# Experts' second layer two pairs of tiles behind the first, with three buffers of h1

## What is computed

```python
x = x + tanh(g_xattn) * attention(ctx, layernorm(x), ctx, mask)
h = layernorm(x) * gamma + beta
shared_out = silu(h @ sw1.T) @ sw2.T
probs = softmax(h @ router_w.T)
best, gate = argmax(probs), max(probs)
routed_out = gate * (silu(h @ ew1[best].T) @ ew2[best].T)
x = x + tanh(g_ffn) * (shared_out + routed_out)
```

## Time and profile before

| | us |
|---|---|
| median of the three runs | 543.09 |
| lowest and highest | 540.36, 544.48 |
| the profiled execution | 543.73 |
| its span, first to last instruction | 541.7 |
| TensorE, VectorE, GpSimd, ScalarE busy in it | 507.2, 435.5, 373.8, 316.1 |
| mean granted clock of TensorE | 0.979 |

### The profile page before, as it was taken

One profiled execution on the slowest core, in us unless ns is written; L12 is line 12 of the kernel. 1 busy time (PEld: TensorE's weight loads), 2 busy tenths in 40 slices (PEclk: granted clock), 3 DMA queues, 4 the chain that ended last, 5 costly groups with the idle time before them and its releaser, 6 DMA issues.

```text
span 541.7 us, 21366 instructions
## 1 busy us (share of the span) xinstructions
PE 507.2 (94%) x8178; PEld 427.4 (79%) x8178; DVE 435.5 (80%) x1257; ACT 316.1 (58%) x711; POOL 373.8 (69%) x828
## 2 busy tenths in 40 slices
PE   6899999999999999999999999999979889999991
PEld 2578677878878788888888888887768879999990
DVE  7688878888898888888777777787677888898971
ACT  3435355555556556666565655645559867777770
POOL 7267888677686777877778677685652777666663
PEclk9799999999999999999999999999979999999996
DMA  6935041020210202112021020200310434232110
GB/s 159 216 105 148 14 136 50 14 59 27 75 56 28 65 25 76 42 43 65 24 76 46 26 65 13 70 12 11 87 47 26 117 105 107 76 85 75 38 40 10
DMA packets 53427, 34.66 MB, mean 64 GB/s; under 512 B 6002, under 2 KB 50750, under 8 KB 53328
## 3 DMA queue, kind: packets, MB, share of 16 engines
q1 hardware_dynamic: 48000, 24.52, 17.1%
q0 software_dynamic: 4320, 8.53, 4.6%
q10 hardware_dynamic: 1008, 0.25, 0.2%
HBM read 24.16 MB, written 9.59 MB: 62 GB/s over the span
## 4 chain that ended last, share of the span: by engine, by line
PE 67%; DVE 16%; POOL 4%; issue 4%; ACT 3%; DMA 2%; SPq 1%; ACTq 0%; POOLq 0%; DVEq 0%
PE PS L1247 11%; PE PS L1215 8%; PE PS L1198 8%; PE PS L1228 7%; PE PS L1185 5%; PE PS L1274 5%; PE PS L1452 5%; PE PS L1456 4%; PE PS L1440 3%; PE PS L1433 3%; DVE nm L629 3%; DVE rinv L637 3%; PE PS L1206 1%; PE PS L1168 1%; PE PS L1285 1%
## 5 line engine op out<-in xcount | busy, mean ns | idle before, releaser
L1016 ACT ACTIVATE shared<-PS 104x768 f32<-104x768 f32 x128 | 103.7, 810 | 52.6 <-PE PS L1228 52.5
L629 DVE TENSOR_REDUCE nm<-PS 128x8 f32<-128x616 f32 x128 | 101.9, 796 | 27.3 <-PE PS L1198 20.6
L1215 PE MATMUL PS<-xT,kbd 32*104 32x128 f32 x1536 | 116.5, 283 | 0.4 <-ACT shared L1016 0.4
L1198 PE MATMUL PS<-kbd,xT 32*128 32x308 f32 x512 | 102.0, 475 | 0.0
L531 POOL DMA_INDIRECT out<-res,tin x71 | 74.0, 1042 | 34.0 <-DVE res L885 19.2
L1215 PEld LDWEIGHTS PS<-xT,kbd 32*104 32x104 f32 x1536 | 89.7, 165 | 1.0 <-ACT shared L1016 0.9
L495 POOL DMA_INDIRECT rows<-X,pos_i x64 | 66.5, 1039 | 29.3 <-DVE X L691 13.4
L637 DVE RECIPROCAL rinv<-PS 128x128 f32<-128x128 f32 x64 | 61.2, 957 | 21.6 <-PE PS L1247 20.6
L1228 PEld LDWEIGHTS PS<-moving,pairsel 128*104 128x104 bf16 x768 | 56.1, 127 | 14.3 <-issue 11.7
L1228 PE MATMUL PS<-moving,pairsel 128*104 128x128 bf16 x768 | 66.2, 222 | 0.0
L1185 PE MATMUL PS<-maskneg,identb 128*128 128x308 bf16 x256 | 55.3, 298 | 3.0 <-DVE nm L629 2.9
(11 more groups left out here) (226 smaller groups left out, 1057.9 us busy)
## 6 DMA issues: line engine op xcount, KB each, us to landing
ctxq<-in_ctx SPq DMA_DIRECT2D x32, 154.0 KB
tin<-rows SPq DMA_DIRECT2D x71, 66.0 KB, 2.0
X<-in_x SPq DMA_DIRECT2D x7, 512.0 KB, 7.1
ctxp<-in_ctx SPq DMA_DIRECT2D x16, 154.0 KB
ctxq<-in_ctx SPq DMA_DIRECT2D x16, 104.0 KB
ctxq<-in_ctx SPq DMA_DIRECT2D x16, 102.0 KB
out<-res,tin POOLq DMA_INDIRECT x71, 2.4
w2n<-in_ew SPq DMA_DIRECT2D x1, 1024.0 KB, 5.8
```

Of the source, the lines that this page charges most:

```text
L629: nc.vector.tensor_reduce(nm[:, b % 2, 2 * u * GH:2 * (u + 1) * GH].rearrange("p (g i) -> p g i", g=2), PS[:, 0:2, 0:GK].rearrange("p g (i ...
L1016: nc.scalar.activation(PT[:, b % 2, 2 * u:2 * u + 2, :], PS[0:CR, 2 + 2 * u:4 + 2 * u, 0:CH * P], ACT.Exp, scale=float(1.0 / np.sqrt(HD))) ...
L1198: ins = nc.tensor.matmul(PS[:, v, 0:GK].rearrange("p (i k) -> p i k", k=SK), xT[r, q % 2, j * P:(j + 1) * P], kbd[r, q % 2, j, :, 0:SK], s ...
L1215: nc.tensor.matmul(PS[0:CR, 2 + g, c * P:(c + 1) * P], kbd[r, q % 2, j].rearrange("p i k -> p (i k)")[:, c * CR:(c + 1) * CR], xT[r, q % 2 ...
```

## The change

h1 gets three buffers instead of two; pair n uses buffer n % 3. The second layer and VectorE's sum go from pair k-1 to pair k-2 of slot k, so that the first two slots of the first group have none, slots 0 and 1 of the other groups take the last two pairs of the group before, and two pairs are left behind the last group. ScalarE's silus wait for the second layer of n-3 instead of n-2. TensorE loads as many experts' numbers into registers as before, and uses four of the group before instead of two. VectorE's split gets a wait for VectorE's own previous split ahead of the tile `rest` being written again.

```diff
@@ buffers
-        h1s = shared[:, 0:4 * F].rearrange("p (s f c) -> p s f c", s=2, f=FB)
-        h1r = shared[:, 4 * F:8 * F].rearrange("p (s a f c) -> p s a f c", s=2, a=2, f=FB)
+        h1s = shared[:, 0:6 * F].rearrange("p (s f c) -> p s f c", s=3, f=FB)
+        h1r = shared[:, 6 * F:12 * F].rearrange("p (s a f c) -> p s a f c", s=3, a=2, f=FB)
@@ VectorE, split
                     dve.wait_ge(h_part, made)
+                ge(dve, split_done, n)
                 nc.vector.tensor_tensor(rest[:, 0:w], hT[:, s, 0:w], hpart[:, s, 0, 0:w], ALU.subtract).then_inc(h_part, 1)
@@ VectorE, group
-                    if k > 0:
-                        combine(g, k - 1)
+                    if k > 1:
+                        combine(g, k - 2)
                     elif not first:
-                        combine(g - 1, SLOTS - 1)
+                        combine(g - 1, SLOTS - 2 + k)
...
                 group(g, first=g == 0, last=g == NG - 1)
+            combine(NG - 1, SLOTS - 2)
             combine(NG - 1, SLOTS - 1)
@@ ScalarE, silus
                 s = k % 2
+                h = n % 3
                 act.wait_ge(zs_psum, n + 1)
-                ge(act, y_psum, n - 1)
+                ge(act, y_psum, n - 2)
...
-                    nc.scalar.activation(h1s[:, s, f, 0:w], PS[:, s, f * 2 * P:f * 2 * P + w], ACT.Silu, scale=wabs[:, E, f:f + 1])
+                    nc.scalar.activation(h1s[:, h, f, 0:w], PS[:, s, f * 2 * P:f * 2 * P + w], ACT.Silu, scale=wabs[:, E, f:f + 1])
...
-                        ins = nc.scalar.activation(h1r[:, s, a, f], PS[:, 2 + s, (2 * a + f) * P:(2 * a + f + 1) * P], ACT.Silu,
+                        ins = nc.scalar.activation(h1r[:, h, a, f], PS[:, 2 + s, (2 * a + f) * P:(2 * a + f + 1) * P], ACT.Silu,
@@ TensorE, second_layer
                 s = k % 2
+                h_ = n % 3
...
-                        nc.tensor.matmul(PS[:, 4 + s, 2 * a * P:(2 * a + 1) * P], h1s[:, s, f, a * P:(a + 1) * P],
+                        nc.tensor.matmul(PS[:, 4 + s, 2 * a * P:(2 * a + 1) * P], h1s[:, h_, f, a * P:(a + 1) * P],
...
-                        ins = nc.tensor.matmul(PS[:, 4 + s, (2 * a + 1) * P:(2 * a + 2) * P], h1r[:, s, a, f],
+                        ins = nc.tensor.matmul(PS[:, 4 + s, (2 * a + 1) * P:(2 * a + 2) * P], h1r[:, h_, a, f],
@@ TensorE, group
-                    before, experts = experts[2:4], experts[4:]
+                    before, experts = experts[0:4], experts[4:]
...
-                    if k > 0:
-                        second_layer(g, k - 1, experts[2 * k - 2:2 * k])
+                    if k > 1:
+                        second_layer(g, k - 2, experts[2 * k - 4:2 * k - 2])
                     elif not first:
-                        second_layer(g - 1, SLOTS - 1, before)
+                        second_layer(g - 1, SLOTS - 2 + k, before[2 * k:2 * k + 2])
...
-                return experts[2 * SLOTS - 2:]
+                return experts[2 * SLOTS - 4:]
...
-            second_layer(NG - 1, SLOTS - 1, spare)
+            second_layer(NG - 1, SLOTS - 2, spare[0:2])
+            second_layer(NG - 1, SLOTS - 1, spare[2:4])
```

## The result

| | before | after |
|---|---|---|
| median, us | 543.24 (22 runs) | 546.45 (22 runs) |
| lowest and highest, us | 540.36, 545.47 | 543.47, 550.21 |
| profiled execution, us | 543.73 | 544.72 |
| its span, us | 541.7 | 542.6 |

The ratio is 1.0055, with a 95% interval of 1.0038 to 1.0071: the change costs 3.2 us, 2.1 to 3.9. The forecast was 545.7 us, 2.6 us more than before: the same by the 1% of the prediction, and slower beyond doubt. The two profiled executions differ by less than the medians, 1.0 us. The work ahead of the experts ended earlier in the second: the first layer of pair 1 starts at 402.28 us instead of 403.18, 0.9 us sooner. From it to GpSimd's last issue the second takes 1.9 us more (131.73 for 129.84).

The account below looks back on a forecast made before the run. The prediction took TensorE's own work, 3.38 us a slot, to bound the full stretch. Its terms, 0 + 0 + 0 + 0 + 2.58 us for the end, added to the median 543.09, gave 545.7 us; range 542.6 to 549.1.

Parts of the forecast that it names:

- The end: Behind the last first layer: two more GpSimd issues lengthen the tail by 2.58 us, with TensorE's 1.88 us inside.
- Slots 2 to 35, no gain and no loss: TensorE's and VectorE's later order in these slots: same work and waits, 0 us a slot.
- Slot 1, free in the gap: Pipeline fill: removing pair 0's second layer gains nothing, leaving one 2.96 us gap set by ScalarE.
- Buffers and added wait, nothing: Third h1 buffer and VectorE's extra split wait: taken as 0 us, the wait at most 0.3 us.
- its stretch from 445 us on: 445 to 527 us, read as slots 12 to 35: TensorE busy 81.93 of 82 us.
- The rival of the clock: Clock falls in slot 1's new gap, costing 1.7 to 3.4 us more: 547.4 to 549.1 us; chance 0.27.
- the lower clock between 407 and 415 us: Sign that the forecast is wrong: TensorE's clock at its low level around and after slot 1's new gap.
- the fall ahead of the stage: Clock fall after 396 us, before the experts' stage; its 6.8 us length was assumed for a fall in the gap.
- VectorE freed: Rival: sums no longer delay VectorE's next splits, saving 3.1 us of first-layer and h1 waits: 542.6 us; chance 0.08.

Follow-up runs that it names:

- e1: Changed kernel with 11 products, results unused, filling TensorE's new gap in slot 1; 545.32 us, ratio 1.0035.
- e4: Changed kernel with TensorE's second layer of pair 0 back in slot 1 and none in slot 2; 544.62 us, ratio 1.0034.
- e6: Changed kernel with ten unused products in the gaps ahead of the experts' stage and eleven in slot 1's new gap; 546.37 us, ratio 1.0040.
- e12: The changed kernel measured again, without further edits, against the kernel before; 546.34 us, ratio 1.0058.
- e10: Changed kernel with the owed second layer paid in slot 34, VectorE's sums following; 546.36 us, ratio 1.0044.
- e3: Kernel before with three h1 buffers, the looser silu wait and the added split wait, order unchanged; 543.87 us, ratio 1.0023.
- e2: Changed kernel with the owed second layer paid in slot 8, one pair behind from then on; 543.83 us, ratio 1.0015.
- e7: Kernel before with VectorE's work on later tiles' tables ahead of its sums in slots 5 to 8; 542.96 us, ratio 0.9979.
- e9: Kernel before with VectorE's sums alone one slot further back in slots 2 to 9, tables ahead, added split wait; 543.03 us, ratio 0.9988.
- e11: Kernel before with VectorE's tables ahead of its sums in slots 5 to 8, measured a second time; 543.47 us, ratio 1.0001.

## Why the prediction was right

**The end** was the one term of the sum, 2.58 us, and it measured 2.58: tails of 9.53 us in all five profiles that keep the debt (after, e1, e4, e6, e12) and of 6.95 us, or 0.01 off, in the eight others that end one pair behind, all but e10. That GpSimd and not TensorE sets it is shown by the changed kernel's last issues, which follow each other without idle time, and by e10: with TensorE's part paid ahead the sum of stretch and tail stayed 2.56 us, not TensorE's 1.88.

**Slots 2 to 35, no gain and no loss**: shown for pairs 12 to 35 (77.63 against 77.65 us) and, while the clock stays, for pairs 1 to 7 (23.91 against 23.92). **Slot 1, free in the gap**: shown by the transposes' place and by e4, which gets 0.21 us for the slot after it. **Buffers and added wait, nothing**: shown for the two stretches of e3 that are as before; for pairs 7 to 12 it is open. One reading of the prediction is loose, without harm: its stretch from 445 us on begins in slot 11, as pair 12 starts at 448.42.

**The rival of the clock was half right, and is not a rival but a part of the result.** Of the four profiles with the gap open, the clock fell in two (e10, e12) and stayed in two (after, e2). The prediction gave it 0.27 and named the lower clock between 407 and 415 us as a sign of being wrong; by that sign it was wrong in half of these profiles. Its price was sized too high: 1.5 us in both, where 1.7 to 3.4 stood. The step that was wrong there is the length: it took that of the fall ahead of the stage, 6.8 us, and here the low level lasted some 3.4 us, of which TensorE worked for about 3.0 us (409.95 to 412.95 in e12). Half of that is 1.5 us, so what is lost is paid in full, as the chain of waits had it. By the Trainium skill (TensorE: Matmul & The Clock Gate, Part 1: the HAM clock gate) the monitor runs freely beside the kernel, so that the point of a transition differs from run to run of one kernel; the two profiles of the changed kernel, one with the fall and one without, fit that.

**What the sum left out** is in pairs 7 to 12: seven profiles of kernels whose TensorE is two pairs behind in these slots (after, e1, e2, e4, e6, e10, e12) take 20.36 to 21.11 us, mean 20.6, seven whose TensorE is one behind 20.83 to 22.58, mean 21.7. So some 1.1 us may come back. That is an estimate from single profiles of different edits, and the two groups overlap; between the kernels before and after themselves it is 0.66 us. Tail, half a clock fall and this are 2.58 + 0.75 - 1.1 = 2.2 us, at the low end of the measured 2.1 to 3.9. So it is partly luck that the total came close: a clock fall that the sum had left to a rival and a gain that it did not have nearly cancel, and 1.0 us of the median's 3.2, though inside its interval, has no cause shown.

The long runs, up to 550.21 us (551.45 in e10), are not the clock's alone. In e12's profile, 549.11 us against 544.72 for the first one of the same kernel, pair 1 starts 3.2 us later (405.48 for 402.28), so that most of the 4.4 us arose ahead of the experts. From there to the last issue it takes 1.2 us more (132.92 for 131.73), with 1.5 us of the clock in it. And e1 and e6, with the gap filled, still had two of twelve runs above 548 us each. One long run in one profile settles no more than that.

**VectorE freed** did not happen in the change: the waits for splits went only from 2.7 to 2.4 us. What it would be worth stays open. Where sums were moved behind other work without the debt, those waits did fall (1.2 us in e7, 1.4 in e9), but others took their place, for a tile in e7 and for a bank in e9, and the time was the same as before.

## What to carry to other kernels

Look first at whether the wait that a deeper pipeline would loosen ever lasts: here it was 0.4 us in the whole run, and the row that said so stood on the first page. Then count what the deeper order moves to the two ends: work taken out of a slot that another engine makes long is not saved there but paid behind the last slot, in the unit of whichever engine drains last (here two issues of GpSimd at 1.29 us, not TensorE's 1.88 us). And where the fill leaves TensorE idle, expect the clock to fall in some runs (here in two of four profiles).

## What was not expected

SyncE writes five stores of padding before it can load pair 9. In the chains of waits before and after, the last of the five:

```profile
425.62 0.66 SPq L346
```

```profile
424.71 0.33 SPq L346
```

In each of the seven profiles with TensorE one pair behind, one of the five (the third, fourth or fifth) took 0.66 to 1.36 us to issue; in the seven with it two behind all were under 0.4 us. GpSimd's and ScalarE's issues around them stand at the same places, to 0.1 us, in the five profiles compared for it. VectorE's longest wait for a tile's rows goes with it: 1.9 us before, 1.7 after, 3.3 in e7. It goes with TensorE's order and not with VectorE's or the buffers (e9 and e3 have it). Why SyncE should feel TensorE's order no run shows; it is left open.

It may be where the gain of pairs 7 to 12 comes from. Before the first layer of pair 8, TensorE transposes pair 9, whose tile SyncE loads behind these stores. From pair 7 to pair 8 the seven profiles with the slow store take 5.06 to 6.81 us, mean 5.9, and the seven others 4.87 to 5.05, mean 5.0, which is most of the 1.1 us. Between the kernels before and after it is 0.22 of the 0.66 us (5.19 and 4.97). The edits of e7, e9 and e11 act on the same slots, so this goes together and is not shown to be the cause.
